# One comparison for the one-hots of four units, two groups ahead, in a ring of sixteen

## What is computed

```python
h = jax.nn.silu(edge_rbf @ W1 + b1)
weights = (h @ W2 + b2).reshape(-1, NODE_DIM, LMAX + 1)
node_j = node_feats[col]
messages = (node_j[:, :, None] * weights).sum(axis=-1)
aggregated = jax.ops.segment_sum(messages, row, num_segments=n_nodes)
```

## Time and profile before

| what | us |
|---|---|
| median of 3 runs | 7541.38 (7531.85 to 7543.0) |
| the profiled execution, its own time | 7546.64 |
| its span, first to last instruction | 7544.8 |
| busy in the span: GpSimd, TensorE, VectorE, ScalarE | 4923.5, 4738.7, 4042.2, 1877.3 |
| mean granted TensorE clock | 0.712 |
| the stage: first one-hot to first start of the last addition | 2322.9 to 2894.6 |

### The profile page before, as it was taken

How to read it: one execution, slowest core, us unless ns; L and a number is a source line. 1 busy time by engine, 2 the same in 40 slices (tenths; PEclk the granted TensorE clock), 3 DMA queues, 4 the chain that set the end, 5 groups by cost and what they waited for, 6 DMA issues and landing times.

```text
span 7544.8 us, 122819 instructions
## 1 busy us (share of the span) xinstructions
PE 4738.7 (63%) x25824; PEld 4062.8 (54%) x25824; DVE 4042.2 (54%) x10081; ACT 1877.3 (25%) x6322; POOL 4923.5 (65%) x5290
## 2 busy tenths in 40 slices
PE   4998999999997889433333433333555555555456
PEld 3777877788777887333333433333444444444333
DVE  7777777777777886533334533334333333333355
ACT  3333333333330001211111111112222222222136
POOL 2777777777773110577777777777777777777730
PEclk8788787777878996555656665666776666666677
DMA  3333333333336774222222222223333333333234
GB/s 102 116 113 113 114 114 116 112 115 113 113 115 190 229 226 106 68 54 54 54 54 54 52 54 54 54 53 58 73 70 71 72 72 74 71 71 70 63 102 127
DMA packets 918696, 698.55 MB, mean 93 GB/s; under 512 B 599463, under 2 KB 782630, under 8 KB 917852
## 3 DMA queue, kind: packets, MB, share of 16 engines
q0 software_dynamic: 163968, 348.11, 16.0%
q1 hardware_dynamic: 263856, 244.54, 11.0%
q10 hardware_dynamic: 490673, 104.07, 7.1%
HBM read 538.76 MB, written 163.86 MB: 93 GB/s over the span
## 4 chain that ended last, share of the span: by engine, by line
POOL 40%; issue 14%; PE 11%; DMA 2%; DVE 1%; DVEq 1%; POOLq 0%; ACT 0%; SPq 0%; ACTq 0%
POOL arena L724 40%; PE bank L1849 6%; DMA arena<-x1d 1%; PE bank L1909 1%; PE bank L1875 1%; DVEq L399 1%; PE bank L1956 1%; DMA arena<-x1d,edge 1%; PE bank L1872 1%; PE bank L1867 0%; PE bank L1873 0%; POOLq L85 0%; PE bank L1955 0%; PE bank L1957 0%; DVE arena L1379 0%
## 5 line engine op out<-in xcount | busy, mean ns | idle before, releaser
L724 POOL DMA_INDIRECT arena<-x1d,edge x3328 | 3164.0, 951 | 1018.2 <-issue 1006.7
L1909 PE MATMUL bank<-arena 128*128 x7040 | 1565.9, 411 | 2277.4 <-SPq L575 1584.6
L1909 PEld LDWEIGHTS bank<-arena 128*128 128x128 f32 x7040 | 1453.8, 315 | 2414.8 <-issue 2414.2
L685 POOL DMA_INDIRECT msgs<-arena x1664 | 1626.7, 978 | 667.2 <-issue 497.7
L1543 DVE TENSOR_TENSOR arena<-bank,arena 128x1024 f32<-128x1024 f32 x440 | 538.5, 1224 | 2125.7 <-PE bank L1909 2054.1
L929 ACT ACTIVATE arena<-edge,arena 128x1 f32 x3520 | 678.2, 280 | 2050.3 <-issue 1929.6
L1807 PE MATMUL bank<-w2s,acc_b 128*128 128x128 f32 x3328 | 675.0, 366 | 0.0
L1807 PEld LDWEIGHTS bank<-w2s,acc_b 128*128 128x128 f32 x3328 | 572.6, 259 | 124.6 <-issue 124.6
L1549 DVE TENSOR_TENSOR acc_b<-acc_b,bank 128x129 f32 x1760 | 508.6, 289 | 210.6 <-PE bank L1909 7.7
L1549 DVE TENSOR_TENSOR acc_a<-acc_a,bank 128x129 f32 x1760 | 508.6, 289 | 210.0 <-PE bank L1909 7.7
L1790 PE MATMUL bank<-arena 128*128 (+1 forms) x3328 | 578.7, 329 | 7.8 <-issue 6.4
(11 more groups left out here) (303 smaller groups left out, 4687.2 us busy)
## 6 DMA issues: line engine op xcount, KB each, us to landing
arena<-rows SPq DMA_DIRECT2D x208, 512.0 KB
arena<-msgs SPq DMA_DIRECT2D x464, 136.0 KB, 3.0
arena<-msgs ACTq DMA_DIRECT2D x464, 136.0 KB, 3.2
arena<-x1d,edge POOLq DMA_INDIRECT x3328
msgs<-arena POOLq DMA_INDIRECT x1664
pred<-arena ACTq DMA_DIRECT2D x98, 256.0 KB, 2.3
arena<-pred SPq DMA_DIRECT2D x12, 1792.0 KB, 8.6
arena<-xwin SPq DMA_DIRECT2D x208, 64.0 KB
```

What stands on the lines that cost most here:

```text
L685: pool.indirect_dma_start(msgs, bass.IndirectOffsetOnAxis(ap=pos[:, b, j:j + 1], axis=0), mrow[:, b, j, :], None).then_inc(scattered[b], 16)
L724: pool.indirect_dma_start(grow_t[:, sl, 0:D], None, x1d, bass.IndirectOffsetOnAxis(ap=edge2[:, odd * RING + sl, 1:2].bitcast(i32), axis=0) ...
L1909: last = mm(sum_at(q, k), oh1[:, q % 2, k, :], grow[:, bass.ds(rows_at[q * TG + k], CW)], start=True, stop=True)
```

## The change

`oh0` becomes a ring of 16 units and moves from the working arena into the first 4,096 words of `acc_b`. One comparison of 128 x 1024 makes the one-hots of a group of four units. It is issued at the head of each group, for the group two later, ahead of the four additions; two such comparisons stand ahead of the first turn. `oh0_ready` now counts groups: TensorE waits for it once in four units, and GpSimd's wait before it writes `local` follows. The matmuls, the additions and their waits, the loads and the table stay as they are.

```diff
-        S0, SO = NS, 8
+        S0, SO = NS, 16
-        oh0 = cut(SO * 2 * P).rearrange("p (s i n) -> p s i n", s=SO, i=2)
+        oh0 = acc_b[:, 0:SO * 2 * P].rearrange("p (s i n) -> p s i n", s=SO, i=2)
...
-                    need(pool, s["oh0_ready"], 4 * n - 4)
+                    need(pool, s["oh0_ready"], n - 1)
...
-            def onehot0(q, k):
-                v.tensor_tensor(oh0[:, (4 * q + k) % SO], iota_row[:, :].rearrange("p (o n) -> p o n", o=1).to_broadcast([P, 2, P]),
-                                local[:, q % 2, k, :].rearrange("p (i o) -> p i o", o=1).to_broadcast([P, 2, P]), ALU.is_equal).then_inc(s["oh0_ready"], 1)
+            def onehots0(q):
+
+                v.tensor_tensor(oh0[:, 4 * (q % 4):4 * (q % 4) + 4].rearrange("p s i n -> p (s i) n"), iota_row[:, :].rearrange("p (o n) -> p o n", o=1).to_broadcast([P, 8, P]),
+                                local[:, q % 2].rearrange("p s (i o) -> p (s i) o", o=1).to_broadcast([P, 8, P]), ALU.is_equal).then_inc(s["oh0_ready"], 1)
...
                 for q in range(NS // 4):
-                    more = not (last and q == NS // 4 - 1)
-                    if more:
-                        dve.wait_ge(s["local_ready"], it * (NS // 4) + q + 2)
+                    if not (last and q >= NS // 4 - 2):
+                        dve.wait_ge(s["local_ready"], it * (NS // 4) + q + 3)
+                        onehots0(q + 2)
                     for k in range(4):
-                        if more:
-                            onehot0(q + 1, k)
-
                         n = 4 * q + k
                         dve.wait_ge(s["sum0_ready"], it * NS + n + 1)
                         need(dve, s["add0_done"], it * NS + n)
...
-            dve.wait_ge(s["local_ready"], 1)
-            for k in range(4):
-                onehot0(0, k)
+            for q in range(2):
+                dve.wait_ge(s["local_ready"], q + 1)
+                onehots0(q)
...
-                    pe.wait_ge(s["oh0_ready"], it * NS + k + 1)
+                    if k % 4 == 0:
+                        pe.wait_ge(s["oh0_ready"], it * (NS // 4) + k // 4 + 1)
```

## The result

The median is 7693.94 us (7690.06 to 7697.13, 4 runs) against 7542.1 before (4 runs); the ratio is 1.0203, with a 95% interval of 1.0191 to 1.0215. The profiled execution took 7694.34 us, with a span of 7692.6, where that of before had 7544.8: 147.8 us more. Lines have moved: the comparison is now L1380, the addition L1394, the matmul L1848.

What follows compares the result with a forecast made beforehand. VectorE was taken to set the pace, TensorE following. From first to last addition 716.5 us against 568.7, +147.8, plus 2.2 at the start, made +150.0 on 7541.4: 7691 us, 2.0% more; range 7645 to 7730.

Steps and rivals of the forecast that it cites:

- The spacing of 0.487: On VectorE, an addition directly following another waits for it: 0.487 us apart, three of four per group, bounds 0.42 to 0.487.
- The sum: VectorE's modelled time from the stage's first addition to its last: 716.5 us against 568.7 measured before, +147.8 us.
- The comparison: On VectorE, one 128x1024 comparison replaces four of 128x256: 1.14 us, bounds 1.07 to 1.23, saving 46 us if nothing else changed.
- The step with the table: VectorE's step between groups holding a table load, 28 times: 2.69 + 1.14 = 3.83 us each, 107.2 in all.
- The start: Ahead of the stage's first addition: later second `local`, then table load and third comparison, delaying that addition by 2.2 us.
- The cover: On VectorE before, a comparison between any two additions hid the wait for the earlier addition; the change removes it.
- Rival one: Additions behind additions do not wait: 0.20 us spacing, group 1.94, total 7494 us; faster below 0.27 spacing; chance 0.05.
- Rival two: TensorE becomes the limit, its clock staying at 1.2 GHz all stage: 807 us, total 7776; chance 0.07 in whole or good part.
- Rival three: Additions run at 0.42 us spacing, 46 us less than forecast: 7645 us, still slower; counted within the forecast's 0.86 chance.

## Why the prediction was right

**The spacing of 0.487 held, and decided.** The sum said 716.5 us from the first to the last addition, and 716.2 were measured. The way it was explained, that the record must end and the semaphore be seen before the next addition is issued, is what the chain of waits shows. The three additions of a group that follow another cost 0.487 each, read off the last four of before; that they were the last did not matter. Moving the wait one addition away took the cost away without touching the instruction; two thirds of the uncovered additions gave two thirds of the loss.

**The comparison held.** 1.14 was forecast, 1.13 to 1.14 measured, in the new place and from two SBUF inputs. The 46 us that it saves are in the trace, and the additions give back four times as much: 696 x (0.487 - 0.20) = 200 us.

**The step with the table** was forecast at 3.83 and is 3.85. A turn is 24.89, forecast 24.9.

**The start** was mis-sized by 0.4 us: 2.2 forecast, 5.61 - 3.02 = 2.6 measured. The second comparison came 2.25 us after the first (2326.51 to 2328.76), where 1.7 was taken from the earlier trace rows: GpSimd wrote the second `local` later, itself waiting for a load of messages. The third came 2.22 after the second, close to the 2.3 taken for the table load; the row puts it down to the third `local`, but that was written at 2330.05. All other stages together came out 2.3 us shorter (147.8 in the span against 147.5 + 2.6). That the total of 150.0 against 147.8 is so close has some luck in it, since single executions differ by more: the runs of the changed kernel span 7 us.

**The cover.** I said that a comparison hid the wait in the kernel before, and inside a turn that is so. At the turn it was not hidden; this did not touch the forecast, since the changed kernel has the same step, but it was there to be found: 2.69 us stand against a load of 2.10.

**The rivals.** Rival one needed a spacing under 0.27; that was measured only once the wait had moved (0.25 in the mean with two accumulators), and the joining then took back what it gained. Rival two did not happen: VectorE waited for sums 8.0 us in all, the same 0.20 under another name, and the clock stayed at 0.93. TensorE stood still for up to 3.2 us a turn, as forecast (3.3), and got the full clock back each time, with 96 us at the low level in the stage against 58 before. Not every gap brings a low stretch: before, one began within 2 us behind 14 of the 28 table loads. Rival three was a real price, 0.417, but for one wait in place of two. GpSimd's L696, of which I said that it might be stretched beside a longer comparison, went from 382 to 208 ns a record. It is stretched beside a comparison, as I said, but it now starts when a comparison has ended and runs beside additions: 229 of its 232 records did so and took 0.20, and the three beside a comparison took 0.60 in the mean. Before, 196 ran beside a comparison and took 0.42.

The lead of two groups is worth no more than some 3 us while VectorE is the limit. Whether it has a use beside the other parts, which bring VectorE near TensorE, was not tried by itself.

## What to carry to other kernels

Before merging small instructions into one, look at what stands between the others afterwards: an instruction put between two dependent ones is free cover, and here taking it away cost four times what the merge saved. The price stands in the trace of before wherever the pattern breaks off, at the end of a loop or in another stage; look for one pair of neighbours without the cover. And work without dependences belongs ahead of a table load, where the engine can do it while its sequencer waits; here that took 38 us off the changed kernel (1.0192 to 1.0142), and nothing that can be told off the order of before.

## What the runs showed of the hardware

- A VectorE addition of 128x128 that waits for the one before starts 0.49 us after it with a second wait on another engine, 0.42 without; with the wait two additions back, 0.19 to 0.29. Behind an addition, an instruction that does not wait for it starts 0.20 after it. With the wait, the sequencer is through with it about 0.06 us after the end of the addition's record, and the next addition starts 0.14 later.
- VectorE works through comparisons already issued while its sequencer spends 2.1 us on a load of 32 registers: two of 1.14 us, issued ahead of the load, lengthened the step from the last addition to the next instruction behind the load from 2.72 to 3.11 us only.
- An f32 comparison costs its engine 0.34 us at 128x256, 0.60 at 128x512 and 1.14 at 128x1024, so 0.07 fixed and 0.27 for each 256 elements; at 128x1024 it is the same from SBUF as with one input in PSUM.
- A GpSimd subtraction of 128x8 took 0.20 us when no comparison ran on VectorE, 0.42 beside comparisons of 128x256 and 0.31 to 0.76 beside those of 128x1024 in the changed kernel.
- TensorE kept the full clock through 400 us with a gap of up to 1.8 us in each turn of 16.4. With 2.3 us in each turn of 19.7 it fell to 1.2 GHz behind half of the gaps, one of them in the earlier trace rows, and with 1.8 us in each turn of 19.0 it still fell twelve times in the stage.
